# First weight slice in halves, warm-ups on a preamble constant, and a new order of the small steps around tile 0

## What is computed

```python
base   = einsum('btd,od->bto', x, W)                       # 512 x 512
logits = einsum('btd,ed->bte', x, Wr) + one_hot(id_b) * 5  # 8 experts
gates  = softmax over the top 2 of logits, 0 elsewhere
h      = einsum('btd,erd->bter', x, A)                     # 8 experts x rank 16
lora   = einsum('bter,bte,eor->bto', h, gates, B)
x + (base + 2 * lora) @ sign * softplus(scale)
```

## Time and profile before

| what | us |
|---|---|
| median of 3 runs | 165.2 (165.15 to 165.34) |
| profiled execution, its own time | 164.64 |
| its span, first to last instruction | 162.8 |
| PE busy | 158.3 (97%) |
| DVE busy | 97.6 (60%) |
| ACT busy | 66.0 (41%) |
| POOL busy | 52.1 (32%) |
| granted TensorE clock, mean | 0.997 of full |

### The profile page before, as it was taken

The page is one execution under the profiler, slowest core; times in us unless marked ns, Lnnn a source line. Parts: engine busy times, 40 slices in busy tenths (PEclk is TensorE's granted clock), DMA queues, the critical chain, the costliest instruction groups (busy, mean ns, idle before and its releaser), DMA issues.

```text
span 162.8 us, 3711 instructions
## 1 busy us (share of the span) xinstructions
PE 158.3 (97%) x1070; PEld 153.8 (94%) x1070; DVE 97.6 (60%) x416; ACT 66.0 (41%) x177; POOL 52.1 (32%) x50
## 2 busy tenths in 40 slices
PE   7999998999999999999999999999999999999993
PEld 5788897999999999999999999999999999999992
DVE  5689997555556665554554555556665555455741
ACT  3654722434344333344444343344333344443440
POOL 2994453332222233333333322222333333333000
PEclk9999999999999999999999999999999999999998
DMA  4996323424333333334333333333333333111113
GB/s 170 380 146 136 90 82 101 131 70 146 105 122 114 124 119 115 124 129 129 129 129 127 104 101 117 112 121 123 113 123 120 128 129 129 64 64 64 68 66 129
DMA packets 29431, 19.51 MB, mean 120 GB/s; under 512 B 7248, under 2 KB 24432, under 8 KB 29424
## 3 DMA queue, kind: packets, MB, share of 16 engines
q1 hardware_dynamic: 28496, 18.23, 36.5%
q10 hardware_dynamic: 928, 1.20, 2.0%
HBM read 11.03 MB, written 8.39 MB: 119 GB/s over the span
## 4 chain that ended last, share of the span: by engine, by line
PE 90%; DVE 7%; issue 1%; ACT 0%; DVEq 0%
PE pair L643 66%; PE pair L679 14%; PE p_b L577 2%; PE p_ht L686 2%; PE pair L589 2%; DVE m_full L470 2%; PE pair L596 2%; PE pair L603 2%; DVE xt L432 1%; DVE wide_lo L476 1%; DVE gate L547 1%; DVE b_lo L501 0%; DVE b_lo L487 0%; DVE wide_lo L483 0%; ACT y L395 0%
## 5 line engine op out<-in xcount | busy, mean ns | idle before, releaser
L300 POOL TENSOR_TENSOR xt_lo<-xt,xt_hi 128x512 fp32r<-128x512 f32 x32 | 41.6, 1299 | 91.5 <-ACT xt_hi L348 91.5
L643 PE MATMUL pair<-wide_hi,xt_hi 128*128 128x392 f32 (+1 forms) x248 | 60.8, 321 | 0.0
L643 PE MATMUL pair<-wide_hi,xt_lo 128*128 128x392 f32 (+1 forms) x248 | 58.3, 311 | 0.0
L643 PE MATMUL pair<-wide_lo,xt_hi 128*128 128x392 f32 (+1 forms) x248 | 58.3, 311 | 0.0
L643 PEld LDWEIGHTS pair<-wide_hi,xt_lo 128*128 128x128 f32 x248 | 38.6, 188 | 0.0
L643 PEld LDWEIGHTS pair<-wide_lo,xt_hi 128*128 128x128 f32 x248 | 38.5, 188 | 0.0
L643 PEld LDWEIGHTS pair<-wide_hi,xt_hi 128*128 128x128 f32 x248 | 38.3, 189 | 0.1
L394 ACT ACTIVATE y<-pair 128x256 f32<-128x256 f32 x31 | 11.9, 384 | 44.3 <-PE pair L679 44.3
L516 DVE TENSOR_TENSOR logits<-pair,bias 128x8 f32<-128x8 f32 x32 | 5.3, 165 | 35.7 <-PE pair L643 35.7
L432 DVE STREAM_TRANSPOSE xt<-x_in 128x512 f32<-128x512 f32 x32 | 22.7, 710 | 3.7 <-DVE top L524 3.2
L348 ACT ACTIVATE xt_hi<-xt 128x512 fp32r<-128x512 f32 x32 | 20.3, 633 | 2.8 <-DVE xt L432 2.8
(11 more groups left out here) (82 smaller groups left out, 142.0 us busy)
## 6 DMA issues: line engine op xcount, KB each, us to landing
x_in<-in_x SPq DMA_DIRECT2D x128, 64.0 KB, 1.9
out<-y SPq DMA_DIRECT2D x31, 256.0 KB, 2.1
sign_in<-in_L_ffn_sign ACTq DMA_DIRECT2D x4, 256.0 KB, 5.1
w_in<-in_L_cond_W SPq DMA_DIRECT2D x4, 256.0 KB, 4.9
a_in<-in_L_cond_A SPq DMA_DIRECT2D x4, 64.0 KB, 5.1
b_in<-in_L_cond_B SPq DMA_DIRECT2D x4, 64.0 KB, 4.2
out<-y SPq DMA_DIRECT2D x1, 128.0 KB, 1.7
out<-y ACTq DMA_DIRECT2D x1, 128.0 KB, 1.8
```

Source lines behind the costliest of these rows:

```text
L300: nc.gpsimd.tensor_tensor(xt_lo[n][:, :, :].rearrange("p j (g b) -> p g j b", g=NQ), xt[n][:, :, :, :], xt_hi[n][:, :, :].bitcast(FP32).re ...
L643: last = nc.tensor.matmul(pair[n][bank][:, at0:at0 + hi - lo], l[:, k, :], w[:, k, lo:hi], start=(opens and k == 0 and l is xt_hi[n] and w ...
```

## The change

1. The fold's slice 0 is handled in halves. ACT makes w_hi of column blocks 0 and 1 (signal first_half_made), then of 2 and 3 (w_hi_made). DVE makes sign_hi of columns 0 to 255 (first_sign_made), then 256 to 511 (early_sign_hi_made). PE makes high_high(0) as four matmuls of 256 columns on the first half of sign, then four on the second; blocks 2 and 3 wait for w_hi_made.
2. Warm-ups: 16, not 18, of the same shape, which read the preamble's bf16 constant 1.0 in place of a tile that DVE zeroes; that tile and its memset are gone.
3. The DMA of scale moves from SP's queue (after x of tile 0) to ACT's, between sign slices 1 and 2, ahead of the table load.
4. Softplus: DVE makes neg_abs between low_w(1) and low_w(2), and the chain of eight between low_w(2) and low_w(3); ACT's Exp and Ln follow sign_hi of slice 2. The transpose of x of tile 0 comes after low_w(3).
5. On ACT b_hi comes before the high parts of the head, and on DVE b_lo before the low parts of the head.
6. In DVE's step 1 (gating of tile 0) b2_lo (low_b2, from step 0) and the transpose of tile 3 come behind h_gated; the wait for bias moves from low_b2 to the start of step 1.

```diff
@@ -42,7 +42,8 @@
     Y0 = D // 2
     BANKS = ((0, 0, HEAD + Y0), (1, HEAD + Y0, WIDE))
     assert BATCH == P and ER == P and D % (NQ * Q) == 0 and HEAD + Y0 <= 512 and O == KC * P
-    WARM_UPS = 18
+    WARM_UPS = 16
+    HALF = D // 2
     EARLY = 1
     S3 = 3
@@ -85,8 +86,6 @@
         b2_hi = sb("b2_hi", [P, D], FP32R)
         b2_lo = sb("b2_lo", [P, D], FP32R)
-        warm_words = sb("warm_words", [P, P])
-        warm = warm_words[:, :].bitcast(BF16)
         ident = sb("ident", [P, P])
         eye = sb("eye", [P, KC, D])
         expert_no_int = sb("expert_no_int", [P, E], INT32)
@@ -131,7 +130,6 @@
         scale_loaded = sem("scale_loaded")
         ids_loaded = sem("ids_loaded")
-        warm_zeroed = sem("warm_zeroed")
         zeroed = sem("zeroed")
         ident_made = sem("ident_made")
         eye_made = sem("eye_made")
@@ -147,6 +145,8 @@
         head_turned = sem("head_turned")
         head_hi_made = sem("head_hi_made")
         head_lo_made = sem("head_lo_made")
+        first_half_made = sem("first_half_made")
+        first_sign_made = sem("first_sign_made")
         w_hi_made = sem("w_hi_made")
         early_sign_hi_made = sem("early_sign_hi_made")
         sign_hi_made = sem("sign_hi_made")
@@ -242,7 +242,6 @@
             for j in range(OC):
                 sp_eng.dma_start(w_in[:, j, :], w_load[:, j, :]).then_inc(w_loaded[j], 16)
             load(0, 0, 0)
-            sp_eng.dma_start(scale_in[:, :], scale.partition_broadcast(P)).then_inc(scale_loaded, 16)
             for i in range(NQ):
                 sp_eng.dma_start(a_in[Q * i:Q * i + Q, :, :], a_load[i, :, :, :]).then_inc(a_loaded, 16)
@@ -328,16 +327,28 @@
             for j in range(OC):
                 act.dma_start(sign_in[:, j, :], sign_load[:, j, :]).then_inc(sign_loaded[j], 16)
+                if j == 1:
+                    act.dma_start(scale_in[:, :], scale.partition_broadcast(P)).then_inc(scale_loaded, 16)
             nc.scalar.preload_act_table_set("natural_log_exp_and_others")
             for j in range(OC):
                 act.wait_ge(w_loaded[j], 16)
-                nc.scalar.activation(w_hi[:, j, :, :, :],
-                                     w_in[:, j, :].rearrange("p (i k a) -> p k i a", i=NQ, k=KC),
-                                     ACT.Copy).then_inc(w_hi_made, 1)
+                w_parts = w_in[:, j, :].rearrange("p (i k a) -> p k i a", i=NQ, k=KC)
+                if j == 0:
+                    nc.scalar.activation(w_hi[:, 0, 0:2, :, :], w_parts[:, 0:2, :, :], ACT.Copy)\
+                        .then_inc(first_half_made, 1)
+                    nc.scalar.activation(w_hi[:, 0, 2:KC, :, :], w_parts[:, 2:KC, :, :], ACT.Copy)\
+                        .then_inc(w_hi_made, 1)
+                else:
+                    nc.scalar.activation(w_hi[:, j, :, :, :], w_parts, ACT.Copy).then_inc(w_hi_made, 1)
                 if j >= EARLY:
                     act.wait_ge(sign_loaded[j], 16)
                     nc.scalar.activation(sign_hi[:, j, :], sign_in[:, j, :], ACT.Copy).then_inc(sign_hi_made, 1)
+                if j == 2:
+                    act.wait_ge(neg_abs_made, 1)
+                    nc.scalar.activation(exp_neg[:, :], sp[:, 0:1], ACT.Exp).then_inc(exp_neg_made, 1)
+                    act.wait_ge(exp_neg_made, 1)
+                    nc.scalar.activation(ln_one[:, :], exp_neg[:, :], ACT.Ln, bias=1.0).then_inc(ln_one_made, 1)
             def high_x(q, r, d, first=False):
                 n = slot(r, d)
@@ -352,19 +363,15 @@
             for i in range(NQ):
                 act.dma_start(wr_in[Q * i:Q * i + E, :], wr_load[i, :, :]).then_inc(wr_loaded, 16)
             act.dma_start(ids_in[:, :], lang_ids.rearrange("(p a) -> p a", a=1)).then_inc(ids_loaded, 16)
-            act.wait_ge(neg_abs_made, 1)
-            nc.scalar.activation(exp_neg[:, :], sp[:, 0:1], ACT.Exp).then_inc(exp_neg_made, 1)
-            act.wait_ge(exp_neg_made, 1)
-            nc.scalar.activation(ln_one[:, :], exp_neg[:, :], ACT.Ln, bias=1.0).then_inc(ln_one_made, 1)
             high_x(0, 0, 0, first=True)
+            act.wait_ge(b_loaded, 16 * OC)
+            nc.scalar.activation(b_hi[:, :, :, :], b_in[:, :, :, :],
+                                 ACT.Copy).then_inc(b_hi_made, 1)
             act.wait_ge(head_turned, 1)
             nc.scalar.activation(wide_hi[:, :, E:HEAD].rearrange("p j (g b) -> p g j b", g=NQ), at[:, :, :, :],
                                  ACT.Copy).then_inc(head_hi_made, 1)
             act.wait_ge(head_turned, 2)
             nc.scalar.activation(wide_hi[:, :, 0:E], wrt[:, :, 0:E], ACT.Copy).then_inc(head_hi_made, 1)
-            act.wait_ge(b_loaded, 16 * OC)
-            nc.scalar.activation(b_hi[:, :, :, :], b_in[:, :, :, :],
-                                 ACT.Copy).then_inc(b_hi_made, 1)
             for k in range(KC):
                 act.wait_ge(m_full_made, k + 1)
                 nc.scalar.activation(wide_hi[:, k, HEAD:WIDE], m_full[:, k, :], ACT.Copy).then_inc(m_hi_made, 1)
@@ -411,7 +418,6 @@
                 ins.then_inc(vec_done, 1)
                 dve.wait_ge(vec_done, chain[0])
-            nc.vector.memset(warm_words[:, :], 0.0).then_inc(warm_zeroed, 1)
             nc.vector.memset(ident[:, :], 0.0).then_inc(zeroed, 1)
             nc.vector.memset(wr_in[:, :], 0.0).then_inc(wr_zeroed, 1)
             nc.vector.memset(eye[:, :, :], 0.0).then_inc(zeroed, 1)
@@ -434,15 +440,14 @@
             for j in range(EARLY):
                 dve.wait_ge(sign_loaded[j], 16)
-                nc.vector.tensor_copy(sign_hi[:, j, :], sign_in[:, j, :]).then_inc(early_sign_hi_made, 1)
+                nc.vector.tensor_copy(sign_hi[:, j, 0:HALF], sign_in[:, j, 0:HALF]).then_inc(first_sign_made, 1)
+                nc.vector.tensor_copy(sign_hi[:, j, HALF:D], sign_in[:, j, HALF:D]).then_inc(early_sign_hi_made, 1)
                 low_w(j)
-            for j in range(EARLY, OC):
-                low_w(j)
-
+            low_w(1)
             dve.wait_ge(scale_loaded, 16)
             nc.vector.tensor_scalar(sp[:, 0:1], scale_in[:, :], -1.0, scale_in[:, 0:1], ALU.mult, ALU.min)\
                 .then_inc(neg_abs_made, 1)
-            turn_x(0, 0, 0, first=True)
+            low_w(2)
             dve.wait_ge(exp_neg_made, 1)
             link(nc.vector.tensor_scalar(sp[:, 1:2], exp_neg[:, :], 1.0, None, ALU.add))
@@ -456,6 +461,8 @@
             link(nc.vector.tensor_scalar(sp[:, 10:11], scale_in[:, :], 0.0, sp[:, 6:7], ALU.max, ALU.add))
             nc.vector.tensor_scalar(sp[:, 11:12], sp[:, 10:11], SCALING, None, ALU.mult).then_inc(softplus_made, 1)
             softplus = sp[:, 10:11]
+            low_w(3)
+            turn_x(0, 0, 0, first=True)
             dve.wait_ge(a_loaded, 16 * NQ)
             nc.vector.transpose(at[:, :, :, :].rearrange("p g j b -> p (g j b)"),
@@ -477,15 +484,15 @@
                                         wide_hi[:, k, HEAD:WIDE].bitcast(FP32), ALU.subtract).then_inc(m_lo_made, 1)
             fold(0)
+            dve.wait_ge(b_hi_made, 1)
+            nc.vector.tensor_tensor(b_lo[:, :, :, :], b_in[:, :, :, :],
+                                    b_hi[:, :, :, :].bitcast(FP32), ALU.subtract).then_inc(b_lo_made, 1)
             dve.wait_ge(head_hi_made, 2)
             nc.vector.tensor_tensor(wide_lo[:, :, 0:E], wrt[:, :, 0:E], wide_hi[:, :, 0:E].bitcast(FP32),
                                     ALU.subtract)
             nc.vector.tensor_tensor(wide_lo[:, :, E:HEAD].rearrange("p j (g b) -> p g j b", g=NQ), at[:, :, :, :],
                                     wide_hi[:, :, E:HEAD].bitcast(FP32).rearrange("p j (g b) -> p g j b", g=NQ),
                                     ALU.subtract).then_inc(head_lo_made, 1)
-            dve.wait_ge(b_hi_made, 1)
-            nc.vector.tensor_tensor(b_lo[:, :, :, :], b_in[:, :, :, :],
-                                    b_hi[:, :, :, :].bitcast(FP32), ALU.subtract).then_inc(b_lo_made, 1)
             fold(1)
             fold(2)
             fold(3)
@@ -496,7 +503,6 @@
             def low_b2():
-                dve.wait_ge(bias_made, 1)
                 dve.wait_ge(b2_hi_made, 1)
                 nc.vector.scalar_tensor_tensor(b2_lo[:, :], p_b2[:, :], sp[:, 11:12], b2_hi[:, :].bitcast(FP32),
                                                ALU.mult, ALU.subtract).then_inc(b2_lo_made, 1)
@@ -510,6 +516,8 @@
             def step(q, r, s):
                 done = S3 * q + r
                 n = slot(r, -1)
+                if s == 1:
+                    dve.wait_ge(bias_made, 1)
                 if has(s, -1):
                     dve.wait_ge(head_ready, done)
@@ -523,10 +531,7 @@
                 if has(s, -1):
                     nc.vector.max(top[:, :], logits[:, :]).then_inc(top_made, 1)
                     dve.wait_ge(top_made, done)
-                if s == 0:
-                    turn_x(q, r, LEAD, first=True)
-                    low_b2()
-                elif has(s, LEAD):
```

(20 more changed lines are left out.)

## The result

The kernel after the change takes 166.19 us (median; 165.41 to 166.77) beside 165.14 for the kernel before on the same chip (164.28 to 165.96): ratio 1.0071, 95% interval 1.0050 to 1.0092. It is **slower by 1.05 us by the medians, 1.17 by the ratio**. The profiled execution took 166.27 with a span of 164.5 (164.64 and 162.8 before). Executions of either kernel scatter by about 1.5 us, so a single profile shows where time can go, and the medians how much goes.

The account below looks back on a forecast made before the run. The prediction took TensorE's matmuls, busy almost throughout, as the bound. It summed -0.88 (hole closed), +0.4 (wait for ht_lo) and +0.8 (POOL first) to +0.3, a median of 165.5 us, range 164.5 to 166.0.

Parts of the forecast that it names:

- Part 1 (gating): Before the transpose of tile 0's gated h: gating ahead of b2_lo closes PE's hole, -0.88.
- the two small instructions before are held too: DVE's gating of tile 0: POOL's xt_lo of tile 2 also delays the instructions before the gate; h_gated ends by 25.65.
- Part 2 (the wait it turns into): Tile 0's lora product: b2_lo and tile 3's transpose, pushed back, make PE wait for ht_lo, +0.4.
- Part 3 (halves): First slice: PE starts near 4.9, but POOL's sign_lo(0) goes first and delays w_lo(0) and low_high(0), +0.8.
- A: Start of slices, the forecast itself: POOL ahead of DVE, low_high(0) 0.7 to 0.9 late; 165.0 to 165.9, chance 0.57.
- Part 4 (softplus, scale): Between slices: moved chain and scale's DMA are covered, w_lo(3) ready by 12.7 against a need at 13.1; zero.
- Part 5 (warm-ups): Before the first product: two fewer warm-ups, PE rests from 4.3 to 4.9; priced at nothing.
- a rise at the same moment: Start of PE's stream: clock level assumed to rise with the first real product, near 5.2, costing only a few halves before it.
- Rival C: First slices: after PE's rest the clock rises later, groups of four take 1.8, not 0.91; 166.4, chance 0.07.
- its sign of being wrong: Slices after 5.3: 512 columns taking 0.43 would show the prediction wrong.

Follow-up runs that it names:

- e3: Kernel before with only the gating order changed (b2_lo and the transpose of tile 3 behind h_gated): 164.28 us, ratio 0.9956.
- e6: Changed kernel with POOL's sign_lo of slice 0 made to wait for w_lo(0), so DVE has the ports first: 165.98 us, ratio 1.0066.
- e17: Kernel before with scale's DMA on ACT's queue after sign slice 1, and POOL's sign_lo(0) waiting for w_lo(0): 166.76 us, ratio 1.0101.
- e11: Kernel before with slice 0 in halves and nothing else: 164.81 us, ratio 1.0015.
- e10: Kernel before with scale's DMA on ACT's queue and the softplus chain between the slices: 166.25 us, ratio 1.0086.
- e5: Changed kernel with the old gating order put back: 166.68 us, ratio 1.0103.
- e1: Changed kernel with 20 warm-ups in place of 16: 165.82 us, ratio 1.0050.
- e18: Changed kernel with scale's DMA, the softplus chain and the turn of x put back, and 20 warm-ups: 163.93 us, ratio 0.9944.
- e7: Changed kernel with b_hi and b_lo back behind the head's high and low parts: 165.90 us, ratio 1.0060.
- e9: Changed kernel with the softplus chain and turn of x back behind the slices, scale's DMA still on ACT's queue: 165.94 us, ratio 1.0084.
- e4: Changed kernel with scale's DMA back on SP's queue: 165.91 us, ratio 1.0050.

## Why the prediction was wrong

The parts are numbered as in the prediction.

*Part 1 (gating), right.* -0.88 for the hole; 0.81 in the profile, and "the two small instructions before are held too" is the case that came: `second` held to 1.10, h_gated in time by 0.63.

*Part 2 (the wait it turns into), too dear.* +0.4 was put for lora waiting for ht_lo; the lora product lost 0.07 in the profile, as h_gated came 0.63 ahead of its need and not 0.29. e3 gains 0.73, not 0.48, but its interval holds both.

*Part 3 (halves), mechanism right, the worth of it not.* Table load 3.1, w_hi at 4.4, first product at 4.86, POOL ahead, w_lo(0) of 1.51, low_high(0) at 6.74: all as forecast (A's 0.66 late, +0.8 was put). But e6 and e17 take the race away and gain 0.0005 of the ratio or nothing. The 0.8 is no term of a sum where another path is as late, be it the clock (e6) or the loads (e17). Also, the fifth issue was filed under the halves; it belongs to scale's DMA, and the halves alone do nothing (e11).

*Part 4 (softplus, scale), the step that failed.* "sign 2 and 3 are issued 0.5 later and have the same cover", w_lo(3) "becomes ready by 12.7", "Zero". The issue was later by 0.5; the landing was later by 3.2 in sign_hi(2), as with scale's 512 bytes in that place the throughput was 68 to 111 GB/s from 5.3 to 6.8 where 318 to 397 was usual. w_lo(3) ended at 14.78. I had counted the DMA as an instruction of its queue and not as traffic ahead of the slices. The second omission is in the same step: neg_abs needs scale, and I didn't ask when it lands. Together they cost 1.4 (e10, 1.1 to 1.8), instead of 0.

*Part 5 (warm-ups), wrong for some executions.* "a rise at the same moment" was the assumption. The rise is at 9.4, 9.1 and 9.4 in the profiles of after, e5 and e6, at 3.6 to 7.2 in all others. Rival C (0.07) described this, its sign of being wrong (0.43 for 512 columns after 5.3) came true in the profile, and its 166.4 lies nearest to the measured 166.19. That nearness is luck: C added 0.9 for the clock to A, while in the medians four more warm-ups return about 0.35, not clear of noise (e1, e18), and e7 and e9, with the rise at 5.1 in their profiles, are 1.0 and 1.4 slower than before by their ratios. The page "TensorE: Matmul & The Clock Gate" of the Trainium skill, Part 1, has this moment shift by 0.5 us either way. The traces do not agree: after and e7 differ only in the order of b and the head, which comes after 15 us, and the rise is at 9.4 in one and 5.1 in the other.

The sum by what was measured: the pair (scale's DMA and the chain) +1.4, gating -0.7, and +0.3 for halves, warm-ups and order of b together, as e5 has them beside the pair and e10 has not (1.0103 against 1.0086, inside the intervals): about +1.0, against 1.05 to 1.17. Each term is uncertain by 0.3 or more, so the agreement shows little. What was missing was a "slower" rival with the right mechanism: a small DMA whose place holds up large ones.

## What to carry to other kernels

Price a moved DMA by what lands behind it, not by its 0.5 us of issue: ask of every transfer that goes ahead of others who waits for the next ones, and try the place alone. The same 128 pieces cost 0.75% between the slices and 0.28% behind them, and passed without a dip on the other queue behind x. Before an instruction is moved forward in an in-order engine, look up when each of its inputs lands. When several parts are changed at once and undoing any one gives little back, two paths may be late together: make the parts alone in the old kernel, in pairs that belong together.

## What the runs showed of the hardware

A DMA of 128 pieces of 4 bytes (scale, one to each partition), issued on ACT's queue between slices of 256 KB, goes with a throughput of 68 to 111 GB/s in the stretch from 5.3 to 6.8 (nine kernels), against 318 to 397 in the eleven kernels without it there. The DMA share is 0.28 to 0.66, against 0.95 or more: the engines are less busy, not more. On SP's queue behind x the same DMA leaves 212 GB/s in its half microsecond, against 179 ahead of it (before). The Trainium skill, page "DMA: Bandwidth & Descriptors", section "Latency and other measured facts", gives 0.2 us as the mean access time of HBM; by an estimate from it, 128 pieces on 16 engines, eight each, one after the other, would take 1.6 us (the same row has 2 us at high load). The hole has about that length, but no run here shows that the pieces are served one after the other, and on SP's queue they seem to pass in about 0.5 us (151 small packets from 8.5 to 9.0). So what makes the hole stays open.

The moment at which PE's granted level goes from 1.2 to 2.4 GHz differed between 3.6 and 9.4 us in single executions of kernels with nearly the same start; the three late ones (over 9) all had 16 warm-ups from 0.76 and a pause of 0.5 before the first product, and e4, e7 and e9, which have them too, were early (5.1 to 5.7).

DVE's `second`, a TENSOR_SCALAR of 8 elements, lasts 1.10 while POOL's TENSOR_TENSOR runs (after, 25.85), where it lasted 0.29 in the kernel before; the gate lasted 1.28 then (24.98) and lasts 0.23 now.
